# Pausing a queue of indirect stores between two halves, and moving a small exponential behind two copies, in a transformer layer on one core

## The reference, cut to what matters

```python
x  = L0_attn_hidden_states                      # (4, 1024, 256)
xn = _layernorm(x)
x  = x + _L0_attn_ref(xn, ...) + _L0_ffn_ref(xn, ...)

# _L0_ffn_ref: 8 experts, the best 2 of each token, and a shared expert
cw = softmax(x @ gate_weight.T), the two largest of each token, scaled to a sum of 1
g  = silu(einsum('th,efh->tef', x, w_gate)) * einsum('th,efh->tef', x, w_up)
y  = einsum('te,teh->th', cw, einsum('tef,ehf->teh', g, w_down))
y  = y + silu(x @ sw_gate.T) * (x @ sw_up.T) @ sw_down.T

# _L0_attn_ref: causal linear attention, and four memories read by the queries
n_f = einsum('bhsd,mhd->mbhs', sq, fine_memory_norms)
w   = softmax(n_f.mean(-1), axis=0)             # one weight per batch, head and memory
out_fine = (outs * w).sum(0)
output = gate * (exp_prob * out_fine + (1 - exp_prob) * out_coarse) + (1 - gate) * local_output
```

## Time and profile before

| | us |
|---|---|
| runs, median of 3 | 712.3 (708.75 to 714.91) |
| profiled execution, its own time | 708.62 |
| its span, first to last instruction | 706.7 |
| granted TensorE clock, mean | 0.956 |

### The profile page before, as it was taken

How to read it: one execution, slowest core, us unless ns; L and a number is a source line. 1 busy time by engine, 2 the same in 40 slices (tenths; PEclk the granted TensorE clock), 3 DMA queues, 4 the chain that set the end, 5 groups by cost and what they waited for, 6 DMA issues and landing times. The chain is left out here.

```text
span 706.7 us, 22451 instructions
## 1 busy us (share of the span) xinstructions
PE 626.9 (89%) x7874; PEld 520.5 (74%) x7874; DVE 509.9 (72%) x1362; ACT 355.9 (50%) x902; POOL 313.4 (44%) x406
## 2 busy tenths in 40 slices
PE   1997869699499999999968999989998999989885
PEld 0785748578399999999956777777776777777663
DVE  3674829358466666666656988889888788888886
ACT  4453625252434444444435766556565475646542
POOL 1153543707481000000030766656675566666775
PEclk9999989989599999999978999999999999999996
DMA  8128271534353333333350012221140202103120
GB/s 283 64 91 277 78 257 56 189 136 149 121 167 116 117 120 118 121 114 117 116 183 34 18 33 92 84 85 32 36 137 29 84 25 65 60 17 92 33 63 32
DMA packets 60123, 71.39 MB, mean 101 GB/s; under 512 B 7612, under 2 KB 55068, under 8 KB 60028
## 3 DMA queue, kind: packets, MB, share of 16 engines
q1 hardware_dynamic: 50956, 52.61, 22.9%
q0 software_dynamic: 6656, 16.86, 7.3%
q10 hardware_dynamic: 2416, 0.59, 0.4%
HBM read 38.45 MB, written 31.59 MB: 99 GB/s over the span
## 5 line engine op out<-in xcount | busy, mean ns | idle before, releaser
L1741 POOL TENSOR_TENSOR tick_a<-lane 128x1 f32<-128x1 f32 x32 | 6.3, 196 | 148.1 <-POOLq L834 145.8
L1744 POOL DMA_INDIRECT yg<-d_grouped_y,from_row x64 | 62.5, 977 | 15.5 <-issue 11.6
L978 ACT ACTIVATE hb<-e_h 88x256 fp32r<-88x256 f32 x72 | 27.5, 382 | 52.7 <-PE e_h L953 52.7
L87 PE MATMUL e_up<-wb,xb 128*128 x144 | 53.0, 368 | 0.5 <-issue 0.5
L1554 ACT ACTIVATE with_mem<-a_ring 128x340 f32<-128x340 f32 x128 | 47.0, 450 | 7.8 <-PE a_ring L1398 7.5
L1010 DVE TENSOR_TENSOR h_sb<-e_up,silu 128x176 f32<-128x176 f32 x72 | 24.6, 342 | 35.3 <-ACT silu L973 35.3
L87 PE MATMUL e_y<-wd,hb 88*128 x146 | 48.7, 334 | 1.0 <-DVE hb L1017 1.0
L1769 POOL TENSOR_TENSOR mem_rows<-mem_rows 128x512 f32<-128x512 f32 x16 | 24.3, 1518 | 54.5 <-DVE mem_rows L1721 54.5
L1681 DVE TENSOR_TENSOR probs<-a_ring,causal 128x256 f32<-128x256 f32 x128 | 45.1, 415 | 3.5 <-remote 3.3
L89 PE MATMUL e_up<-wb,xb 128*128 x144 | 46.9, 326 | 0.0
L88 PE MATMUL e_up<-wb,xb 128*128 x144 | 46.9, 326 | 0.0
(11 more groups left out here) (300 smaller groups left out, 2069.7 us busy)
## 6 DMA issues: line engine op xcount, KB each, us to landing
xg<-d_rows SPq DMA_DIRECT2D x77, 128.0 KB, 2.0
d_grouped_y<-y_sb SPq DMA_DIRECT2D x73, 128.0 KB, 1.8
d_base<-xn_in SPq DMA_DIRECT2D x8, 512.0 KB
xn_in<-d_xn SPq DMA_DIRECT2D x4, 1024.0 KB
total<-d_base SPq DMA_DIRECT2D x8, 512.0 KB
out<-total SPq DMA_DIRECT2D x7, 512.0 KB, 3.3
mem_rows<-in_w_up SPq DMA_DIRECT2D x4, 704.0 KB
v<-in_x_tok SPq DMA_DIRECT2D x2, 1024.0 KB
```

The costliest lines, as they stand in the source:

```text
L87: pe.matmul(out, a[0], b[0], start=start, stop=False)
L978: act.activation(hb[o][0][:, :, :], ps_h[o][0:FC, 0:2 * P].rearrange("p (k n) -> p k n", k=2), ACT.Copy).then_inc(s_hh, 1)
L1744: pool.indirect_dma_start(yg[tile % GATHERS][:, k, :], None, d["grouped_y"], bass.IndirectOffsetOnAxis(ap=c["from"][:, k, tile:tile + 1], ...
```

## The change

Two independent edits. In the tokens phase POOL waits between its eighth and ninth row store of a batch (b = 2, 3 and 4) until all four pieces of the next batch's transposed rows are split. In the attention phase `mexp` stands behind `values` and `gate` in the first tile of a batch, and `weights` stands in the second tile, behind the scores and ahead of `coef`. (The line that defines `by_memory` is repeated so that `weights` has it.)

```diff
@@ tokens_phase, gpsimd
                     for t in range(NT):
+                        if t == TS and b <= B:
+                            pool.wait_ge(s_xl, (b + 2) * NS * KC)
                         for k in range(TOP):
                             pool.indirect_dma_start(
@@ attention_order
         order += [("scores", b, t, j) for j in range(4)]
         if i > 1:
             order.append(("outT", *tiles[i - 2], 0))
+        if t == 1:
+            order.append(("weights", b, 0, 0))
         if i:
             order += [("coef", *tiles[i - 1], 0), ("rest", *tiles[i - 1], 0)]
...
         if t == 0:
-            order += [("mean", b, 0, 0), ("mexp", b, 0, 0)]
+            order.append(("mean", b, 0, 0))
         order += ahead + [("values", b, t, 0), ("values", b, t, 1)] + behind + [("gate", b, t, 0)]
+        if t == 0:
+            order.append(("mexp", b, 0, 0))
...
         if t < NT - 1:
             order.append(("state", b, t, 1))
-        if t == 0:
-            order.append(("weights", b, 0, 0))
```

More of the change, by code:

```diff
@@ L1651, in walk @@
                     elif what == "weights":
+                        by_memory = mw[:, :, :, :].rearrange("p g n r -> p g r n")
                         since(dve, s_mexp, b + 1)
```

## The result

The changed kernel took 689.27 us (median of 4, 685.24 to 692.86) where the kernel before took 711.22 (median of 4 on the same chip): ratio 0.969, 95% interval 0.961 to 0.976, 22 us less. The profiled executions are 685.24 and 708.62, 23.4 apart; 685.8 was predicted. The sum came out, but its two terms did not: the later runs show what each is worth, and that the larger one is worth nothing on another chip.

A forecast was written before the change was run, and what follows sets the result against it. PE, busy 89% of the span, was taken as the bound, with time won where it idles or runs at its lower clock. Pause 20.5 plus exponential 6.0 made 26.5, taking 712.3 to 685.8; range 682 to 708.

The forecast's parts named there:

- The second residual, `hidden(1)`, POOL's ninth store: First batch boundary, tokens phase: residual at 52.9, split done about 55.3, ninth store some 3.7 late, PE idle below 0.5.
- The stores as the cause: Tokens phase: PE's signals seem held while POOL issues the second half of a batch's stores; inferred from timing.
- The pause: Three batch boundaries of the tokens phase: 22.5 of PE time regained, less 2 for loading x, so 20.5.
- I take nothing: Tokens phase: the second half of the stores, moved behind the pause, was taken to hold no signals, at no cost.
- rival (a): Tokens phase: second half of stores still holds signals, 3 lost per boundary; pause worth 11.5, total 694.8; chance 0.28.
- the 2 for the x load: Tokens phase: the next batch's x has less cover, costing 1 at each of two boundaries.
- The exponential: Attention phase: copies to `valT` start when `values` ends; PE regains 7.1, less 1.1, so 6.0 (bounds 1.6 and 7.1).
- the 1.1 that I took off for `outT` behind POOL: Attention phase: PE waits for POOL before `outT`, 0.2 per batch and 0.5 in the first.
- The lower bound of 1.6: Attention phase: least gain from moving the exponential and weights, only DVE's 0.4 in each batch.
- The sum: Whole kernel: 20.5 in the tokens phase plus 6.0 in attention, 26.5 in all, from 712.3 to 685.8; chance 0.47.
- rival (b): Tokens phase: stores are not the cause, split still ends at 60.2; only the 6.0 remain, 706.3; chance 0.12.

The follow-up runs named there:

- B: The second chip of the follow-up runs: the kernel before took 715.83 there (706.49 to 725.77, 13 executions).
- C: The third chip of the follow-up runs: the kernel before took 707.58 there (698.6 to 714.2, 7 executions).
- A: The first chip of the follow-up runs, not that of the first comparison: the kernel before took 681.9 there in 17 executions.

## Why the prediction was right, and where it was not

**The second residual, `hidden(1)`, POOL's ninth store.** Right, at each step and to some tenths: residual at 53.13 (52.9 predicted, in a trace that runs 0.2 later), split done 55.49 (55.3), pause 3.92 (3.7), idle of PE none.

**The stores as the cause.** Right for B, shown there by leaving stores out (195.57 and 193.38 against 167.72); for the first chip and C it is argued from the same pattern in their traces. The Trainium skill's rule in "SBUF — State Buffer", section "Who interferes with whom", that "PE and ACT never wait on anyone", speaks of access to the memory's ports. What I drew from it, that the stores can't cause the gaps, holds on A and fails on B, where PE's result reaches DVE 10.8 late beside the stores and at once without them. Whether a port has a part in it no run shows.

**The pause: 20.5 predicted, 15.1 measured.** The step that failed is "I take nothing, because the silent 3.7 us put it in the position of a first half rather than of a continued one". The second half still held the second logits until 1.6 behind its last store. PE paid 1.88, 1.88 and 0.93 ahead of the ranks, 0.81 each behind them, and twice a stretch at a clock of 0.68. Against the even 31.82 of a batch on B without these stores, the three boundaries lose 9.6 in all (22.7 before). That is rival (a), at its price of 3 a boundary. The term comes out only 5 below the forecast because two things make up for part of it: 2.2 in the last batch, which the pause doesn't touch, and the 2 for the x load. That a silence resets anything is not shown. The x load, taken at 2, cost nothing seen: DVE's statistics start at 61.22 and 97.11, 0.3 behind DVE's operation before them and not released by the load.

**The exponential: 6.0 predicted, 8.8 measured on the first chip, 13 on A.** The mechanism was right, but two sizes were off. I costed PE's idle by its length alone. By the start of each batch's third pair of copies to `valT` (400.48, 483.31, 567.44 and 650.57 before; 384.47, 465.49, 546.35 and 627.34 after, each from the start of the phase at 362.28 and 347.65) the four batches gain 1.4, 1.8, 3.3 and 2.1. The clock was 1.00 behind the idle in all but the third, where it was 0.87, and there the gain is some 1.4 more. On A the kernel before has dips of some 2.9 twice in one trace. And the 1.1 that I took off for `outT` behind POOL came only in part: PE waits 0.68 for `att` in the second tile of the first batch and shows no idle at that place in the other three (its wait for `att` goes from 3.8 to 5.1 in all, the rest of it in the last batch). The lower bound of 1.6 stood on "only DVE's 0.4 in each batch"; without the `weights` moved, a batch gains 0.3 where there is no dip, which is 1.2 in all four, below that bound.

**The sum.** 26.5 predicted, 23.4 between the traces, 22 between the medians: 5 too much in one term, 3 too little in the other. That it came so near is partly luck. The 9.6 that I put at nothing are in large part made up for by the x load, which I had as a cost of 2, by 2.2 in the last batch and by 2.8 in attention, which the sum didn't have; what is left are differences of some tenths. On A the pause is worth nothing, as in rival (b), but not by its mechanism: (b) has the split late for another reason, and on A it isn't late. And attention brings 13 there instead of 6.

**What the prediction could not see.** I took a held signal for a property of the kernel. One trace can't show that it differs between chips. The range (682 to 708) held for the changed kernel on the chip of the comparison; on A it takes 667.38, and the kernel before is already at 682.

**Left open.** What makes the signals late on one chip and not on another, and whether it is the chip or the state it was in at the time (B and C were used once, A twice within minutes); whether the number of stores in a row counts or where they stand (the run meant for it paused too little); whether it is the traffic or POOL's issuing (the run meant for it fell on a chip that doesn't hold). The traces name no releaser.

## What to carry to other kernels

An idle of PE costs its length and the dip in the clock that may follow, here 1.4 to 2.9 behind 1.8: read the granted clock behind each gap before pricing it. A wait that is taken away at one place can come back at the next: look at the distance from batch to batch, and not only at the gap that was meant. When an engine's signals come late with no releaser in the trace, look whether a row of indirect stores is beside them, and run the kernel before on a second chip before building on it. When a step is taken out of one engine's way, look at its followers too: the exponential without its five followers gave back 1.6 of each batch.

## What the runs showed of the hardware that was not expected

The same kernel took 682 on one chip and 708 to 716 in three comparisons elsewhere. In the two traces of it, 25.6 of the 28.8 between them lie in the tokens phase (experts phase from 165.3 on A and 190.9 in the first trace; from 193.4 and 195.6 in two kernels with the same tokens phase on B). What differs is how late PE's signals reach DVE and ACT while POOL issues indirect stores: not at all on A for DVE's second residual, 2.4 in the first trace and 10.8 on B for the same instruction. It differs within a chip too: the unbroken row of the last batch held ACT's product to its end in the first trace, and not in the trace of the changed kernel. Where a signal is held to the end of the row it arrives 1.5 to 2.5 behind the last store's end (1.5 twice, 1.6 twice, 2.0, 2.5). The kernel before also spreads more on the chips that hold: 19 us over 13 executions on B, 15.6 over 7 on C, 5.7 over 17 on A.
